# A graph layer and an expert layer in one kernel: early expert results stored in item order and gathered per tile, and a reordered tail

## The reference, cut to what matters

```
N, D, E, H = 12500, 256, 8, 512        # nodes, features, experts, hidden; 212500 edges sorted by dst
xn  = layernorm(x)
agg = segment_sum(xn[src] * edge_weight[:, None], dst, N)      # gather of rows, scaled, summed per node
x   = x + agg @ gnn_W.T + gnn_b
xf  = layernorm(x)
p   = softmax(xf @ gate_w + gate_b); keep the two largest of 8 per node, with their probabilities
y   = sum over the node's 2 experts e of p[e] * (gelu(xf @ W1[e] + b1[e]) @ W2[e] + b2[e])
out = x + y
```

## Time and profile before

| | |
|---|---|
| runs of the kernel before | 2648.48, 2654.87, 2655.98 us; median 2654.87 |
| the profiled execution | 2653.09 us, span 2651.2 us |
| granted TensorE clock, mean of the span | 0.898 of full speed |
| gathers of rows on POOL | 1664 indirect DMAs in 208 groups |
| scatters of results on POOL | 224 indirect DMAs, 1 KB rows |
| copies of runs on SP | 784 DMAs of 136 KB |
| HBM traffic | 548 MB read, 210 MB written |

### The profile page before, as it was taken

How to read it: one execution, slowest core, us unless ns; L and a number is a source line. 1 busy time by engine, 2 the same in 40 slices (tenths; PEclk the granted TensorE clock), 3 DMA queues, 4 the chain that set the end, 5 groups by cost and what they waited for, 6 DMA issues and landing times.

```text
span 2651.2 us, 47128 instructions
## 1 busy us (share of the span) xinstructions
PE 2118.5 (80%) x11356; PEld 1664.7 (63%) x11357; DVE 1464.6 (55%) x6118; ACT 664.3 (25%) x1932; POOL 1819.5 (69%) x1905
## 2 busy tenths in 40 slices
PE   4666776698689699987788789799898887996595
PEld 3444454476477577765566566577777766775485
DVE  7888454465365364464466375364556565574243
ACT  2332121122122123222122122123232222322232
POOL 7666777777777777777777777777777776770021
PEclk8767898899899899998889899899999988998798
DMA  8766846867758768858879868869788887985596
GB/s 290 242 199 213 250 141 190 262 205 240 238 187 256 251 205 283 287 175 275 279 223 315 269 210 273 257 190 319 256 259 284 286 281 248 322 267 165 168 369 220
DMA packets 304874, 652.64 MB, mean 246 GB/s; under 512 B 61364, under 2 KB 196182, under 8 KB 291926
## 3 DMA queue, kind: packets, MB, share of 16 engines
q1 hardware_dynamic: 171812, 356.59, 40.0%
q0 software_dynamic: 90624, 247.58, 30.7%
q10 hardware_dynamic: 42162, 45.37, 4.9%
HBM read 548.25 MB, written 210.23 MB: 286 GB/s over the span
## 4 chain that ended last, share of the span: by engine, by line
PE 27%; POOL 24%; DVE 14%; issue 13%; DMA 11%; SPq 9%; DVEq 1%; ACT 1%; ACTq 0%; POOLq 0%
POOL rows L450 22%; PE bank L783 9%; PE bank L876 8%; SPq L568 6%; PE bank L860 6%; DMA slots<-stage 5%; POOL results L477 2%; DMA results<-y_sb,result_i 2%; DVE spread L1237 2%; DMA rows<-xhat,src_t 1%; DVE bn L1216 1%; DMA xi<-slots 1%; DMA stage<-sorted_x 1%; PE bank L803 1%; PE bank L811 1%
## 5 line engine op out<-in xcount | busy, mean ns | idle before, releaser
L450 POOL DMA_INDIRECT rows<-xhat,src_t x1488 | 1425.9, 958 | 468.4 <-issue 448.5
L783 PE MATMUL bank<-rows,spread 128*80 128x256 f32 x3328 | 890.1, 428 | 222.7 <-DMA rows<-xhat,src_t 151.2
L783 PEld LDWEIGHTS bank<-rows,spread 128*80 128x80 f32 x3328 | 557.7, 171 | 517.5 <-issue 187.6
L876 PE MATMUL bank<-w,hT 128*128 x1792 | 457.5, 401 | 53.0 <-DVE y_sb L1448 33.0
L860 PEld LDWEIGHTS bank<-xiT,w 128*128 128x128 f32 x3584 | 442.8, 195 | 32.5 <-DMA w<-in_w 8.7
L860 PE MATMUL bank<-xiT,w 128*128 128x128 f32 x3584 | 446.8, 279 | 12.2 <-DMA w<-in_w 7.0
L876 PEld LDWEIGHTS bank<-w,hT 128*128 128x128 f32 x1792 | 339.5, 200 | 111.2 <-issue 69.5
L1250 DVE TENSOR_TENSOR acc<-acc,bank 128x160 f32 x208 | 66.9, 322 | 616.8 <-PE bank L773 557.0
L1054 ACT ACTIVATE hT<-bank,b1T 128x128 f32<-128x128 f32 x896 | 255.8, 368 | 597.2 <-PE bank L860 523.7
L477 POOL DMA_INDIRECT results<-y_sb,result_i x224 | 222.6, 994 | 259.7 <-DVE y_sb L1448 206.4
L1237 DVE TENSOR_SCALAR spread<-iota_w,dst_rel,wgt 128x80 f32<-128x80 f32 x1488 | 365.2, 339 | 0.1
(11 more groups left out here) (175 smaller groups left out, 1694.7 us busy)
## 6 DMA issues: line engine op xcount, KB each, us to landing
w<-in_w SPq DMA_DIRECT2D x224, 512.0 KB
slots<-stage SPq DMA_DIRECT2D x784, 136.0 KB
xi<-slots SPq DMA_DIRECT2D x224, 136.0 KB, 4.7
stage<-sorted_x ACTq DMA_DIRECT2D x98, 272.0 KB
rows<-xhat,src_t POOLq DMA_INDIRECT x1488
got<-results SPq DMA_DIRECT2D x73, 256.0 KB, 5.6
x_t<-in_x SPq DMA_DIRECT2D x97, 128.0 KB
x_d<-x_t ACTq DMA_DIRECT2D x97, 128.0 KB
```

The source lines that it names most:

```text
L450: pool.indirect_dma_start(rows[q][:, c, :], None, x if g < RAW else xhat, bass.IndirectOffsetOnAxis(ap=src_t[:, g * CG + c:g * CG + c + 1] ...
L783: done = nc.tensor.matmul(B_SUM[0:W, 0:D], spread[g % 2][:, c, :], rows[q][:, c, :], start=c == 0, stop=c == CG - 1)
L876: done = nc.tensor.matmul(bank[:, 0:D], hT[i % 2][:, j, :], w2[:, bass.ds(e, 1), j, :].rearrange("p o f -> p (o f)"), start=j == 0, stop=j ...
```

## The change

Results of the first three epochs (items 0 to 188, `FIRST_LATE` = 189) are no longer scattered. ACT stores the 128 rows of y as they stand to `yq`, item after item, one turn after the result (`store_y`, list `queued`). The list of each epoch's blocks goes to DRAM and comes back broadcast to 128 partitions. For each tile DVE turns block and row within the block into a row of `yq` (`index_results`, and ten small operations more in `place` to keep block and row). POOL gathers the two rows of each node by two indirect DMAs per tile (`gather_results`), three turns after the index in busy turns. In a busy turn ACT's `store_y` stands between `exponent` and the gelu of the first step, and DVE's `index_results` behind `combine` and ahead of `softmax`, `choose`, `place` and the turn's second result. SP keeps the load of x1. Results of the last epoch are still scattered.

The order behind the last gather changes too. The last epoch is cut as (4, 4, 2, 2, 2) instead of (4, 4, 4, 2). A tail turn may hold two linears and two gates (`linear2`, `gate2`), and PE, ACT and DVE take the calls of a tail turn in another order. There are 16 tail turns instead of 17. The 8 run copies of tiles 92 to 97 are split, experts 0 to 3 on SP and 4 to 7 on POOL. The last 14 tiles are combined four at a time, by operations of 1024 columns.

Counted from the two planners: POOL issues 35 scatters instead of 224, and 168 result gathers (60 in turns 107 to 136, 64 in turns 175 to 206, 44 in turns 212 to 217).

```diff
-EPOCH_SIZES = ((6, 8, 8, 8), (8, 8, 8, 8), (8, 6, 4, 4), (4, 4, 4, 2))
+EPOCH_SIZES = ((6, 8, 8, 8), (8, 8, 8, 8), (8, 6, 4, 4), (4, 4, 2, 2, 2))
+FIRST_LATE = FIRST_ITEM[-2]
+SHARED = (range(0, 4), range(4, 8))
...
+                if with_sums and not busy and lin < NT:
+                    t.linear2 = lin
...
-            t.results += [s[0] for s in back.steps if s[0] >= 0 and s[0] not in result_at]
+            t.results += [s[0] for s in back.steps if s[0] >= FIRST_LATE and s[0] not in result_at]
+            t.queued = [s[0] for s in turns[-1].steps if 0 <= s[0] < FIRST_LATE]
...
+        def runs_done(eng, t):
+            shared = max(0, t - FIRST_SHARED)
+            if t:
+                eng.wait_ge(runs_in, 16 * (NX * (t - shared) + len(SHARED[0]) * shared))
+            if shared:
+                eng.wait_ge(pool_runs_in, 16 * len(SHARED[1]) * shared)
+        def copy_some_runs(eng, t, done):
...
+            for e in SHARED[done is pool_runs_in] if t >= FIRST_SHARED else range(NX):
...
+                eng.dma_start(slots[bass.ds(b, P), :], stages[t % STAGES][bass.ds(a, P), :]).then_inc(done, 16)
...
+            def results_done(t):
+                last = FIRST_ITEM[EPOCH_OF[PART_OF[t]] + 1]
+                for q in range(YB):
+                    pool.wait_ge(y_kept[q], block_moves(q) + 16 * len(range(q, last, YB)))
+            def gather_results(t, to, done):
+                if t in EPOCH_TILES:
+                    results_done(t)
+                pool.wait_ge(indexed, t + 1)
+                for c in range(2):
+                    pool.indirect_dma_start(to[:, c, :], None, yq[0:FIRST_ITEM[EPOCH_OF[PART_OF[t]] + 1] * P], bass.IndirectOffsetOnAxis(ap=gather_i[:, t, c:c + 1], axis=0)).then_inc(done, 16)
...
                     for i in t.results:
                         scatter_result(i)
+                    for u in ([t.stage] if t.stage >= 0 else []) + t.quick:
+                        if u >= FIRST_SHARED:
+                            copy_some_runs(pool, u, pool_runs_in)
+                    if t.batch >= 0:
+                        gather_batch(plan, t, fast, first_batched)
+                    elif t.busy:
+                        for u in t.fetches:
+                            if u >= CB:
+                                pool.wait_ge(res_ready, u - CB + 1)
+                            gather_results(u, got[u % CB], got_in[u % CB])
...
-                sp.dma_start(got[b][0:n], result_pairs[t * P:t * P + n]).then_inc(got_in[b], 16)
...
+            def store_y(i):
+                act.wait_ge(y_ready, i + 1)
+                act.dma_start(yq[i * P:(i + 1) * P], y_sb[i % YB][:]).then_inc(y_kept[i % YB], 16)
...
+                    for i in t.queued:
+                        store_y(i)
...
-                    dve.wait_ge(y_out[i % YB], 16 * (i // YB))
+                    if i - YB < FIRST_LATE:
+                        dve.wait_ge(y_kept[i % YB], block_moves(i % YB) + 16 * (i // YB))
+                    else:
+                        dve.wait_ge(y_out[i % YB], late_stores(i % YB, i))
-                nc.vector.tensor_copy(result_i[i % YB][:], xi[i % XI][:, bass.ds(e + C_ID, 1)]).then_inc(result_i_ready, 1)
+                if i >= FIRST_LATE:
+                    nc.vector.tensor_copy(result_i[i % YB][:], xi[i % XI][:, bass.ds(e + C_ID, 1)])
...
+            def index_results(t):
+                m = EPOCH_OF[PART_OF[t]]
+                if t in EPOCH_TILES:
+                    dve.wait_ge(list_moved, 32 * (m + 1))
+                here = slice(FIRST_ITEM[m], FIRST_ITEM[m + 1])
+                hit = item_hit[:, 0:EPOCH_ITEMS[m]]
+                for c in range(2):
+                    then(nc.vector.scalar_tensor_tensor(hit, item_all[:, here], block_of[:, t, c:c + 1], item_row[:, here],
+                                                        op0=ALU.is_equal, op1=ALU.mult))
+                    then(nc.vector.tensor_reduce(item_of[:, c:c + 1], hit, axis=AX.X, op=ALU.add))
+                then(nc.vector.tensor_tensor(item_of[:], item_of[:], row_of[:, t, :], op=ALU.add))
+                nc.vector.tensor_copy(gather_i[:, t, :], item_of[:]).then_inc(indexed, 1)
...
+                    for u in t.index:
+                        index_results(u)
...
+                if m == LATE_BATCH and t1 < NT and j // LATE_BATCH < R:
+                    nc.vector.tensor_tensor(to, to, of[:, :, 0], op=ALU.add).then_inc(half_added, m)
+                    dve.wait_ge(half_added, t1)
+                    nc.vector.tensor_tensor(to, to, of[:, :, 1], op=ALU.add).then_inc(res_ready, m)
```

More of the change, by code:

```diff
@@ L182, in plan @@
                 gate += 1
+                if with_sums and not busy and gate < NT and lin_at.get(gate, tau) < tau and PART_OF[gate] == k:
+                    t.gate2 = gate
+                    gate_at[gate] = tau
+                    gate += 1
         for k in range(NK):
@@ L232, in plan @@
         for back in turns if not busy else turns[:-1]:
-            t.results += [s[0] for s in back.steps if s[0] >= 0 and s[0] not in result_at]
+            t.results += [s[0] for s in back.steps if s[0] >= FIRST_LATE and s[0] not in result_at]
         if turns:
             t.combines, t.stores = turns[-1].fetches, turns[-1].combines
+            t.queued = [s[0] for s in turns[-1].steps if 0 <= s[0] < FIRST_LATE]
         stored += len(t.stores)
-        for i in t.results:
+        for i in t.queued + t.results:
             result_at[i] = tau
+        for k, at in listed_at.items():
+            if ends_epoch(k) and EPOCH_OF[k] < NE - 1:
+                if at == tau - 1:
+                    t.list_store = EPOCH_OF[k]
+                if at == tau - 2:
+                    t.list_load = EPOCH_OF[k]
+        if t.listing >= 0:
+            listed_at[t.listing] = tau
+        while index_next < LATE and len(t.index) < (1 if busy else BATCH):
+            if not result_at.get(FIRST_ITEM[EPOCH_OF[PART_OF[index_next]] + 1] - 1, tau) < tau:
+                break
+            index_at[index_next] = tau
+            t.index.append(index_next)
+            index_next += 1
         all_sent = sent_at.get(NK - 1, tau) < tau
@@ L241, in plan @@
         while fetch_next < LATE and len(t.fetches) < most:
-            m = EPOCH_OF[PART_OF[fetch_next]]
-            if not result_at.get(FIRST_ITEM[m + 1] - 1, tau) < tau - (2 if busy else 0):
+            if not index_at.get(fetch_next, tau) < tau - (2 if busy else 0):
                 break
@@ L264 @@
 (PLAN, FIRST_BATCHED), (PLAN_GENERAL, GENERAL_BATCHED) = plan(True), plan(False)
+FIRST_SHARED = min(u for t in PLAN if not t.busy for u in ([t.stage] if t.stage >= 0 else []) + t.quick)
 TWO_BANKS = min(step[1] for t in PLAN[NG + 2:] for step in t.steps if step[1] >= 0)
 def freed_before(g):
-    return sum(t.linear >= 0 for t in PLAN[:g + 2])
+    return sum((t.linear >= 0) + (t.linear2 >= 0) for t in PLAN[:g + 2])
 for _g in range(NG):
@@ L357, in build @@
         node_rows = [rows[2][:, i, :] for i in range(CG)] + [a[:] for a in res]
+        late_pairs = [rows[i // 4][:, i % 4 * 2:i % 4 * 2 + 2] for i in range(R * 4)] + [a[:] for a in got]
+        assert CG == 2 * LATE_BATCH and len(late_pairs) >= NT - LATE
         TB = len(pairs)
@@ L1065, in tail_turn @@
                     copy_xnT(t.gate)
+                for i in t.queued:
+                    store_y(i)
+                for _, b, _, _ in t.steps[:1]:
+                    if b >= 0:
+                        gelu(b, fast)
+                if t.gate2 >= 0:
+                    copy_xnT(t.gate2)
+                for _, _, c, _ in t.steps[:1]:
+                    if c >= 0:
+                        copy_xiT(c)
+                if t.linear >= 0:
+                    normalise(t.linear)
+                    store_x1(t.linear)
                 if t.choose >= 0:
                     exponent(t.choose)
[L1068 removed]
+                if t.sums >= 0:
+                    copy_sums(t.sums)
+                for _, b, c, _ in t.steps[1:]:
                     if b >= 0:
@@ L1481, in tail_turn @@
                     fold(t.linear // RING, group_of_tile(t.linear) + 1)
+                for u in (t.linear, t.linear2):
+                    if u >= 0:
+                        add_x(u)
                 if t.linear >= 0:
-                    add_x(t.linear)
                     node(t.linear, fast)
+                if t.place >= 0:
+                    place(t.place)
+                for a, _, _, _ in t.steps[:1]:
+                    if a >= 0:
+                        result(a, fast)
                 if t.softmax >= 0:
```

167 lines of the change are left out of this document (113 added, 54 removed).

## The result

The change made the kernel slower by half a per cent: 2668.3 us (median of 6 runs, 2665.01 to 2674.04) against 2653.4 us (median of 6 runs, 2648.48 to 2658.14). The ratio is 1.0051, with a 95% interval of 1.0032 to 1.0071. Forecast were 2592 us and a range of 2550 to 2638. The profiled execution has a span of 2671.1 us and a granted clock of 0.897 of full speed, which is the 0.898 of before.

A forecast was written before the change was run, and what follows sets the result against it. GpSimd's queue, without pause from 283 to 1994 us, was taken as the bound, PE close behind. Terms: -35-16+7 = -44 up to the last gather, -17 behind it, so 2653.1-61 = 2592 us; range 2550 to 2638.

The forecast's parts named there:

- the floor under each stage: Stage length less PE's row waits, taken as PE's limit: 378, 461, 302, 420 and 408 us for stages one to five.
- VectorE's additions: Index operations per tile and in place: 126 and 33 us of work, mostly covered; +7 us taken, bounds 0 and 130.
- Slots of GpSimd: GpSimd's queue before the last gather: 1.256 us per DMA, 63 slots (79 us) freed, only -35 us of time.
- Stages one, two and four: Turns 22-64, 64-106, 136-174: fewer GpSimd DMAs shorten them by 24, 25 and 18 us, PE's floor bounding two and four.
- the y waits: VectorE's waits for scatter landings holding y buffers, stages two and four, go: 12 and 4 us gained, -16 together.
- Stage three: Turns 106-136: 60 result gathers added on GpSimd make it 32 us longer.
- rival C: Slower: VectorE's additions delay softmax, choose and second results, PE's down waits for y; 2715 us priced in full; chance 0.11.
- the two signs I had named: PE's waits for y_sb or xnT growing by tens of us would show VectorE's additions deciding the time.
- Stage five: Turns 174-207: 64 result gathers leave GpSimd at 404 us against PE's 408, so 0 us change.
- Behind the last gather: After 2402 us: -26 from reorder with sharing (sharing -7), +9 for later items, new gathers taken as 0; sum -17.
- D: Result gathers slow (1.37 us plus gap, +51) or the tail's 44 in the open (+55): 2643 to 2647 us; chance 0.07.
- A: PE's floors hold, nothing is relieved, y waits hidden by PE's work, tail gives nothing: 2625 us; chance 0.18.

The follow-up runs named there:

- run 3: Kernel after the change without VectorE's index work (index_results and the ten operations in place), a constant list gathered: 2621.6 us, ratio 0.9875 to the kernel before.
- run 1: Kernel after the change with four more 136 KB run copies per tile on SyncE, into a spare buffer, for tiles 0 to 83: 2818.2 us, ratio 1.0629.
- run 2: Kernel after the change without the result gathers of tiles 0 to 61, VectorE adding rows of b2B instead: 2625.2 us, ratio 0.9889.
- Run 5: Kernel before the change with seven y buffers instead of four: 2653.8 against 2653.1 us, ratio 0.9999.
- run 4: Kernel after the change with the run copies of tiles 0 to 91 split, four on SyncE and four on ScalarE: 2800.7 us, ratio 1.0567.
- run 9: Kernel after the change with the W1 loads of busy turns issued by ScalarE instead of SyncE: 2688.6 us, ratio 1.0135.
- run 6: Kernel after the change with tiles 0 to 29 fetched every other turn from 107 to 165, not every turn from 107 to 136: 2638.2 us, ratio 0.9951.

## Why the prediction was wrong

The step that failed is the floor under each stage. I took a stage's length, subtracted PE's waits for rows, and called the rest what PE needs: 461 us for stage two, which then took 479.3. That assumes that rows in time bring no other wait. But where tiles are sent, a chain of another queue needs nearly as long as GpSimd did: 10.65 us a turn in the part above, where GpSimd's eight gathers need 10.05 and with a scatter 11.3. Among PE's waits of before that chain hardly shows, since GpSimd was late as well. SyncE's own waits show it, for the landing of the tile before, 18 times from 283 to 731 us and 13 times from 731 to 1217 of the kernel before:

```profile
SPq L562 <- DMA slots<-stage: 35.6, 18, 3.3
...
SPq L562 <- DMA slots<-stage: 20.3, 13, 3.5
```

I had read its parts, 14.80 us for two tiles and one landing, and used them only behind the last gather. They would have given 8.7 us a tile (6.05 and 2.69), less than GpSimd's 10.05; in the stages with gathers the landing is 4.6. In stage two PE's row waits of 25.2 us did go, as the step has it, and the stage lost 5.9. The 13.1 us of them around the part above brought nothing: the wait for xi there rose from 7.2 to 17.8 us. The 12.1 us behind it brought 7.6. VectorE's additions cost 11.4 us in this stage by run 3: 2 ahead of the part, some 10 behind the first new xi, none between.

Point by point:
- **Slots of GpSimd.** 1.256 us per slot, the gather count by stage and the 0.96 us of a result gather all hold (median 946 ns, as in the earlier trace rows). The gathers' mean stayed at 956 ns (958 before) beside 123 us more of VectorE's work.
- **Stages one, two and four:** -24, -25, -18 taken, and with the y waits -83 in all; measured -14.9, -5.9, -3.4, which is -24. PE's waits for rows fell from 151.2 to 97.7 us over the span, and those for xi rose from 77.6 to 99.6. In stages two and four GpSimd stood 58.4 and 49.3 us for row buffers, so its freed slots had no taker there. Run 1 shows that a longer send chain costs in these stages; by how much they would shrink with a shorter one isn't shown. The -3.4 of stage four is inside the 4 us to which a stage is known.
- **Stage three:** +32 taken, +31.9 measured, and run 2 gives 37.1 of it back. This is the part where GpSimd was the bound and stayed it; PE's row waits in it rose from 37.2 to 61.4 us, where I expected them near zero outside stage one.
- **The y waits:** -16 taken. Run 5 takes them away in the kernel before and gains 0, within 4 us.
- **VectorE's additions:** +7 taken (0 to 130 as bounds); run 3 measures 47 us with their share of the tail. This is a mis-sized term, and a part of rival C: a third of the work is exposed. The work itself was 135 us where 126 and 33 were taken; the parts that `place` serves are 12, not the 13 of the prediction. Of the two signs I had named, PE's waits for y_sb fell (33.0 to 23.6 us), and those for xnT grew from 40.0 to 54.9, but they are 54.3 without the index too. The work cost time ahead of the sends and behind the last gather.
- **Stage five:** 0 taken and 4 for VectorE; +12.9 measured. Without the index it is 9.9 us less; the 3.1 less without the gathers are inside the 4 us. The index was the cost, and I had it at 4.
- **Behind the last gather:** the part ahead of the items came as forecast, 92 us for 91. The 44 gathers and 22 indices in it were taken as covered; with the items that enter later they cost 23.5 where 9 were taken. Run 3 takes 17.7 us out of this part, so it is the index rather than the gathers that is in the open. The sharing was worth somewhat more than 7.
- **Rivals.** None gave the number; D's 2647 is nearest, by another cause. A comes nearest in kind (nothing relieved, y waits hidden), but it kept the floors. C gave the sign. In D the price of a result gather was wrong at the 1.37 us it assumed, and the 64 of stage five cost nearly nothing.

That the send chain took over in the part at 795 us is shown by its 10.65 us in both kernels, by SyncE's wait for a landing at each tile, by the lead that stayed at 12 us through it, and by run 1. It doesn't pace all sends: in the next part it waited at two tiles of seven, and PE was the bound. The stretch between the two parts' sends (119.7 us before, 120.9 after) is 20 us until the first new xi, in which PE mostly stands, and then PE's own work, busy 91.59 of 99.86 us before and 91.71 of 100.41 after. The two attempts to make the chain shorter, runs 4 and 9, took issues to an engine that stands in the same loop, and lost without making its cycle shorter. So how the 10.65 us divide into issue (6.0) and landing (what is left, 4.65) in what they cost was measured on the side of more issues only, and what a shorter chain would gain stays open. Shorter copies were not tried. It is open too where in the loop of ScalarE the 20 us of run 9 arise.

## What to carry to other kernels

When an engine with no idle time is relieved, ask which other chain would need nearly as long per turn, and measure its cycle from the trace: the distance of its own starts from turn to turn shows it, and so do the waits of the queue that issues it. The waits of the engine it feeds do not, so long as the first engine comes last. Ask it for each stretch by itself, since the next bound changed within one stage here. Work that is moved into a few turns should be spread over turns in which its new engine has time: the same 124 gathers cost 43 us where 60 of them were bunched and some 13 when these were spread (runs 2 and 6). Small operations on a half idle engine are free only if they don't stand ahead of a chain's first step.

## What the runs showed of the hardware

- A direct DMA with register offsets costs GpSimd 0.49 us and 0.18 us behind it, an indirect one 946 ns and 0.30 us; SyncE needs 0.52 us and 0.25 us for the former.
- Sets of eight 136 KB copies from DRAM to DRAM landed 3.5 to 6.2 us behind the start of their last issue. The mean of eight sets was 4.64 us with GpSimd's scatters beside them and 4.65 without, and 4.29 (of seven) with twelve copies in a set.
- Four more copies of 136 KB per tile cost next to nothing (0.2 us) in a stage of 12.4 us per turn, where the turns without a send made up for them, at a DMA share of 0.83, and 1.7 to 2.6 us per tile in the others.
- Issues moved to ScalarE, which is busy 25%, cost 132 us when those of a tile waited for a landing (run 4) and 20 us when they did not (run 9).
